# Attention as 64x64 quarter-array products of one head and two images (ViT tower, one core)

## What is computed

```python
B, N, D, H, DH = (64, 17, 256, 16, 64)       # images, tokens, width, heads, head width
q = (x @ Wq).reshape(b, n, H, DH)            # k, v alike
bias = slope[:, None, None] * (pos[:, None] - pos[None, :])
scores = jnp.einsum('bihd,bjhd->bhij', q, k) * scale + bias[None]
scores = jnp.where(causal[None, None], scores, jnp.float32(-1e+30))
attn = jax.nn.softmax(scores, axis=-1)
out = jnp.einsum('bhij,bjhd->bihd', attn, v).reshape(b, n, H * DH)
return out @ Wo + bo
```

## Time and profile before

| | before |
|---|---|
| median of 3 runs | 598.27 us (597.21 to 599.42) |
| profiled execution: time / span | 600.16 us / 598.4 us |
| mean granted TensorE clock | 0.918 |
| PE busy (MATMUL) / PE weight loads | 502.0 us (84%) / 405.5 us (68%) |
| DVE / ACT / GpSimd busy | 432.8 / 336.7 / 218.1 us |
| score products, L911: MATMUL records | 512, from 211.0 to 321.8 us |
| value products, L944: MATMUL records | 512, from 229.1 to 338.8 us |

### The profile page before, as it was taken

One profiled execution on the slowest core, in us unless ns is written; L12 is line 12 of the kernel. 1 busy time (PEld: TensorE's weight loads), 2 busy tenths in 40 slices (PEclk: granted clock), 3 DMA queues, 4 the chain that ended last, 5 costly groups with the idle time before them and its releaser, 6 DMA issues.

```text
span 598.4 us, 10880 instructions
## 1 busy us (share of the span) xinstructions
PE 502.0 (84%) x3750; PEld 405.5 (68%) x3754; DVE 432.8 (72%) x995; ACT 336.7 (56%) x798; POOL 218.1 (36%) x230
## 2 busy tenths in 40 slices
PE   3988953175654899999998998989999999999795
PEld 2756842033322789999998887867777777777584
DVE  4988998999999366666666323757686777766665
ACT  1588625245554867777775247336676767767500
POOL 2110001022222622222221522376777777777500
PEclk9996987577875899999999999999999999999969
DMA  8990000007400000000000010106777778887492
GB/s 266 380 359 0 1 0 0 0 2 250 115 2 1 1 27 29 28 29 28 27 2 3 1 53 23 29 13 191 225 219 217 219 229 237 232 240 213 133 398 80
DMA packets 43897, 67.36 MB, mean 113 GB/s; under 512 B 11022, under 2 KB 27015, under 8 KB 43716
## 3 DMA queue, kind: packets, MB, share of 16 engines
q1 hardware_dynamic: 36868, 64.62, 33.9%
q0 software_dynamic: 6976, 2.07, 1.8%
HBM read 66.81 MB, written 17.20 MB: 140 GB/s over the span
## 4 chain that ended last, share of the span: by engine, by line
PE 60%; DVE 24%; ACT 5%; issue 4%; DMA 3%; POOL 2%; SPq 0%; DVEq 0%; POOLq 0%; ACTq 0%
PE ps L1090 11%; PE ps L733 7%; PE ps L735 6%; PE ps L734 6%; PE ps L954 5%; PE ps L740 5%; PE ps L911 3%; PE ps L944 3%; PE ps L1080 3%; PE ps L926 2%; PE ps L1137 2%; PE ps L1098 2%; DVE region L1727 2%; DMA region<-x_rows,region 2%; DVE region L1738 2%
## 5 line engine op out<-in xcount | busy, mean ns | idle before, releaser
L1090 PE MATMUL ps<-region 128*128 128x352 f32 x256 | 86.4, 460 | 0.3 <-issue 0.3
L684 POOL DMA_INDIRECT region<-x_rows,region x64 | 67.9, 1061 | 20.2 <-issue 15.8
L733 PE MATMUL ps<-nTh,high 128*128 128x272 f32 (+2 forms) x248 | 73.7, 297 | 0.4 <-ACT region L1365 0.4
L734 PE MATMUL ps<-nTl,high 128*128 128x272 f32 (+2 forms) x248 | 71.1, 287 | 0.0
L693 POOL DMA_INDIRECT y_rows<-region x60 | 61.9, 1031 | 21.0 <-issue 14.4
L1783 DVE TENSOR_TENSOR region<-ps,region 32x136 f32<-32x136 f32 x128 | 38.1, 297 | 39.0 <-PE ps L911 37.5
L643 POOL COPY region<-region 32x544 f32<-32x544 f32 x32 | 26.1, 815 | 95.2 <-DVE region L1802 93.7
L1931 DVE SCALAR_TENSOR_TENSOR region<-region,ps 128x176 f32<-128x176 f32 x64 | 25.4, 397 | 44.7 <-ACT region L1442 42.9
L735 PE MATMUL ps<-nTh,pairs_low 128*128 128x272 f32 x192 | 55.0, 287 | 0.0
L1090 PEld LDWEIGHTS ps<-region 128*128 128x128 f32 x256 | 43.6, 190 | 14.1 <-issue 0.5
L1452 ACT ACTIVATE high<-region 88x512 fp32r<-88x512 f32 x64 | 40.4, 631 | 22.5 <-PE ps L735 21.5
(11 more groups left out here) (264 smaller groups left out, 1329.8 us busy)
## 6 DMA issues: line engine op xcount, KB each, us to landing
region<-moe_w SPq DMA_DIRECT2D x64, 352.0 KB, 3.9
region<-moe_w SPq DMA_DIRECT2D x64, 176.0 KB
y_rows<-zrow SPq DMA_DIRECT2D x1, 6528.0 KB, 25.5
region<-y_rows SPq DMA_DIRECT2D x8, 768.0 KB, 10.6
region<-wqkv SPq DMA_DIRECT2D x8, 384.0 KB, 3.0
region<-ffn_w SPq DMA_DIRECT2D x2, 1024.0 KB, 8.2
region<-patches SPq DMA_DIRECT2D x3, 384.0 KB, 8.3
region<-patches SPq DMA_DIRECT2D x1, 1152.0 KB, 10.7
```

What stands on the lines that cost most here:

```text
L684: nc.gpsimd.indirect_dma_start(out=xb[m8], out_offset=None, in_=x_rows, in_offset=bass.IndirectOffsetOnAxis(ap=sloti[:, at:at + 1], axis=0 ...
L733: nc.tensor.matmul(out, parts_a[0], parts_b[0], start=first, stop=False)
L734: nc.tensor.matmul(out, parts_a[0], parts_b[1], start=False, stop=False)
L1090: mm = nc.tensor.matmul(ps[:, 2 + m % 2, 0:2 * EI], xbT[m % 2][:, c, :], w13[m][:, c, :], start=(c == 0), stop=(c == DC - 1))
```

## The change

The score products become products of one head and two images: 64 partitions, 64 stationary and 34 moving columns. The keys are kept as they come out of the projection (`kT`), without zeros. Each half of the scores has its own two banks, one per head. The value products become products of one head and two images as well: 64 partitions (two images x 32 padded keys), 64 stationary and 34 moving columns, with `pbd` block-diagonal over two images; two banks are filled at a time, one per pair of images. There are twice as many products, each a quarter of the array. ACT's, DVE's and GpSimd's addresses follow. The `reg2.cut` lines without a name keep the places of the other buffers.

```diff
-        kbd = reg2.cut([P, GT, 2, GW])
+        kT = reg2.cut([P, N])
+        reg2.cut([P, 2 * GT * GW - N])
...
-        pbd = [reg2.cut([P, 2 * GT, GW]) for _ in range(2)]
+        pbd = [reg2.cut([P, 2 * GT, 2 * T]) for _ in range(2)]
+        reg2.cut([P, 2 * GT * GW])
...
-            nc.gpsimd.memset(kbd, 0.0).then_inc(s_zero, 1)
...
-            pool.wait_ge(s_zero, 6)
+            pool.wait_ge(s_zero, 5)
...
-                    nc.gpsimd.tensor_copy(pbd[j][r, :, q * T:(q + 1) * T], prT[r, :, 0:T]).then_inc(s_spread, 1)
+                    nc.gpsimd.tensor_copy(pbd[j][r, :, (q % 2) * T:(q % 2 + 1) * T], prT[r, :, 0:T]).then_inc(s_spread, 1)
...
                     def scores(half):
 
-                        need(pe, s_ext, 2 * n + half)
+                        need(pe, s_ext, 2 * n + half - 1)
                         for g in range(8):
                             t = 8 * half + g
-                            for u in range(2):
-                                mm = nc.tensor.matmul(ps[64 * u:64 * u + 64, 4 + g // 2, (g % 2) * GW:(g % 2 + 1) * GW].rearrange(
-                                                          "p (h w) -> p h w", h=2),
-                                                      qT[:, 4 * t + 2 * u:4 * t + 2 * u + 2, :].rearrange("p b t -> p (b t)"),
-                                                      kbd[:, t, :, 2 * u * T:2 * (u + 1) * T], start=True, stop=True)
+                            for hd in range(2):
+                                f = slice(DH * hd, DH * hd + DH)
+                                for u in range(2):
+                                    b = 4 * t + 2 * u
+                                    mm = nc.tensor.matmul(ps[64 * u:64 * u + 64, 4 + 2 * half + hd, 2 * g * T:2 * (g + 1) * T],
+                                                          qT[f, b:b + 2, :].rearrange("p b t -> p (b t)"),
+                                                          kT[f, b * T:(b + 2) * T], start=True, stop=True)
                         mm.then_inc(s_qk, 1)
...
-                    for g in range(4):
-                        if project and g == 2:
+                    for half in range(2):
+                        if project and half == 1:
                             scores(1)
-                        b = fill(g if not project else 16 + g)
-                        for k in range(4):
-                            for hd in range(2):
-                                f = slice(DH * hd, DH * hd + DH)
-                                mm = nc.tensor.matmul(ps[f, b, k * GW:(k + 1) * GW], vp[1 - j][:, 4 * g + k, f],
-                                                      pbd[1 - j][:, GT * hd + 4 * g + k, :], start=True, stop=True)
-                        mm.then_inc(s_fill, 1)
+                        at = 2 * half if not project else 16 + 2 * half
+                        banks = (fill(at), fill(at + 1))
+                        for k in range(8):
+                            for u in range(2):
+                                r = slice(64 * u, 64 * u + 64)
+                                for hd in range(2):
+                                    f = slice(DH * hd, DH * hd + DH)
+                                    mm = nc.tensor.matmul(ps[f, banks[u], 2 * k * T:2 * (k + 1) * T],
+                                                          vp[1 - j][r, 8 * half + k, f],
+                                                          pbd[1 - j][r, GT * hd + 8 * half + k, :], start=True, stop=True)
+                                if k == 7:
+                                    mm.then_inc(s_fill, 1)
...
-                            for hd in range(2):
-                                f = slice(DH * hd, DH * hd + DH)
-                                ins = nc.scalar.activation(kbd[f, 4 * q:4 * q + 4, hd, :],
-                                                           ps[f, q, 0:CW].rearrange("p (g w) -> p g w", w=GW), ACT.Copy)
-                            ins.then_inc(s_evac, 1)
+                            nc.scalar.activation(kT[:, q * CW:(q + 1) * CW], src, ACT.Copy).then_inc(s_evac, 1)
...
-                        nc.scalar.activation(attnT[:, n - 1, 4 * g * GW:4 * (g + 1) * GW], ps[:, g, 0:4 * GW],
-                                             ACT.Copy).then_inc(s_evac, 1)
+                        half, u = g // 2, g % 2
+                        nc.scalar.activation(
+                            attnT[:, n - 1, 8 * half * GW:8 * (half + 1) * GW].rearrange("p (k u w) -> p k u w", k=8, u=2)[:, :, u, :],
+                            ps[:, g, 0:16 * T].rearrange("p (k w) -> p k w", k=8), ACT.Copy).then_inc(s_evac, 1)
...
-                                sc[r, s0:s0 + 8, 0:T].rearrange("p (a b) t -> p a b t", a=4),
-                                ps[r, 4:8, 0:2 * GW].rearrange("p a (b h t) -> p a b h t", b=2, h=2)[
-                                    :, :, :, hd, (q % 2) * T:(q % 2 + 1) * T],
-                                bc(bc(bias[r, :], 1, 2), 1, 4), ALU.add)
+                                sc[r, s0:s0 + 8, 0:T],
+                                ps[r, 4 + 2 * half + hd, 0:16 * T].rearrange("p (g w) -> p g w", g=8)[
+                                    :, :, (q % 2) * T:(q % 2 + 1) * T],
+                                bc(bias[r, :], 1, 8), ALU.add)
```

More of the change, by code:

```diff
@@ L918, in attention @@
                     if n == 0:
-                        pe.wait_ge(s_zero, 6)
+                        pe.wait_ge(s_zero, 5)
                     scores(0)
@@ L1806, in _ @@
             low_parts(2, 0, len(groups))
-            dve.wait_ge(s_zero, 6)
+            dve.wait_ge(s_zero, 5)
             dve.wait_ge(s_wo1, 48)
```

## The result

The changed kernel takes 605.0 us (median of 6 runs, 603.07 to 607.65) where the kernel before takes 598.24 (6 runs, 596.79 to 599.42): ratio 1.0114, 95% interval 1.0096 to 1.0131. The forecast was 595.0 in a range of 591 to 623: the time is inside the range and on the other side of no change.

What follows compares the result with a forecast made beforehand. The attention loop was taken as bound by TensorE's own stream; -2.4 - 0.8 - 0.6 + 0.45 = -3.3 us on the profiled 600.16 gave 596.9, with the median 1.9 lower: 595.0 beside 598.27, range 591 to 623.

Steps and rivals of the forecast that it cites:

- R2: Score and value blocks: instruction feed gives 17 to 19 ns a pair, block 1.1 to 1.2 us, 602 to 605; chance 0.13.
- (a): Score and value blocks: 16 slots of 55 ns, 0.88 us instead of 0.94, with shorter block ends: -2.4 us together.
- R1: Score and value blocks: row halves take turns, 32 slots, 1.76 us a block, 623 us; chance 0.14.
- R2b: Score and value blocks: feed already at its limit, 29 ns a pair, 1.86 us a block, 626 us; chance 0.06.
- R4: Score and value blocks: load quicker in a quarter tile, down to 30 ns a slot, 583 us; chance 0.05.
- R3: Score and value blocks: tiles overlap but the slot stays near 59 ns, nothing measurable, 597 us; chance 0.12.
- (b): Scores half 1 of n=0: a bank pair per half removes the wait for DVE's read of half 0: -0.8 us.
- (c): Keys leave PSUM in four copies instead of eight, shortening PE's waits for ACT at n=1: -0.6 us.
- (d): Drain pass: value blocks free two banks at their end, so PE waits for two copies instead of one: +0.45 us.
- (e): POOL's clearing before attention is about 3.8 us shorter, its copies and DVE's reads move as much as before: nothing.

Runs made afterwards that it cites:

- one-image run: The changed kernel with 17 moving columns a product instead of 34, the odd image of each pair not computed: 609.98 us, one execution, beside before's 597.93.
- shifted kernel: The changed kernel with 64 transposes of a bf16 identity (128 instructions) added where TensorE waits for DVE, long before attention: 605.48 us, ratio 1.011.
- two joined versions: Kernel before with two banks per scores half, both halves behind the twelfth projection group: 0.9978; the same with quarter scores and keys without zeros: 0.9941.
- values alone: Kernel before with the changed kernel's quarter value products, probabilities and attnT copies, scores and keys as before: 603.18 us, ratio 1.0081.
- scores alone: Kernel before with the changed kernel's quarter scores, keys and DVE reads, value products as before: 598.66 us, ratio 0.9998.

## Why the prediction was wrong, step by step

**The step that failed is the feed of instructions.** The sum puts it at nothing; it stands beside the sum as R2. The prediction saw that the change needs a pair per 14 ns, and asked of the trace only how fast TensorE takes the pairs of one block; it gave this 0.13, as an even slowing to 17 to 19 ns a pair. The runs showed in its place two rates: within a piece of instructions the feed keeps up with 14.5 ns a pair (128 pairs in 1.85 us), and pieces of 256 instructions cannot follow each other faster than some 3.5 us. So nothing is slower in most blocks, and 0.5 to 2.2 us is lost at once in others. That R2's 602 to 605 holds the measured 605.0 is luck: the mechanism is another. A row that could have raised the question was on the page of before and wasn't read, the instruction queue. It shows how many pieces come, not how fast they could; the same stretch, 240 to 256 us, in before and then in after:
```profile
q8 instruction: 1, 0.02, 0.5%
```
```profile
q8 instruction: 3, 0.05, 1.3%
```
Before needs 436 instructions an iteration of 15.1 us, after 693 (both counted in the traces). On average 693 would still arrive in 9.5 us; it is the run of 384 within 2.8 us that outruns them. What makes the next piece start is open: in the changed kernel's attention it mostly starts 0.6 to 1.6 us after TensorE enters a new piece, but sometimes before that, and once 3.1 us after. That one belongs to the longest stop, 2.23 us at 261.55: the last piece had been entered at 257.9, and the next packet started only at 261.0. So I can't say ahead which iteration stops.

**(a), the blocks, -2.4 forecast, none measured.** The mechanism was right: four quarter tiles overlap, 16 slots a block. The size was off: 58 ns a slot, not 55, so 0.93 us a block, where the forecast had 0.88 and the kernel before 0.94 to 0.95. The two block ends of an iteration gave some 20 to 30 ns each, as forecast: score block to transposes is 1.07 instead of 1.10 us, the last value block to the projections 1.07 instead of some 1.11. So the four blocks of an iteration took 0.09 us less, not 0.30. And the rest took it back: an undisturbed iteration is 15.12 to 15.19 us against 15.12; the projections with their neighbours took 9.20 us (232.21 to 241.41) instead of 9.13, which no run explains. The one-image run shows that the forecast's reason, streaming sets 59 and the load 55, was half wrong: with 17 columns the slot is 58 too, so the stream does not set it, and whatever does costs 58 and not 55. The load itself is as forecast, a median of 135 ns with 64 rows, 136 with 128. By the Trainium skill ("TensorE: Matmul & The Clock Gate", LDWEIGHTS (loading the stationary operand)) it goes with columns only; the trace agrees.

R1 (turns, 1.76 us a block) and R2b (1.86) fall to the same 0.93, R4 too. The floor of about 25 ns between MATMUL starts that the Trainium skill gives ("TensorE: Matmul & The Clock Gate", "Wait — 56ns, not 53.3ns?") does not hold for four tiles: 64 starts in 0.93 us are 14.5 ns apart. R3's place, a slot near 59, is what the array part did.

**(b), n = 0, -0.8 forecast.** Transposes to scores half 1 is 1.90 us (212.23 to 214.13) instead of 2.74: -0.84. Right.

**(c), the keys, -0.6 forecast.** The rest of the first iteration's -1.49, -0.65; the stop of 0.67 us before L733 at n = 1 is gone. The two joined versions differ by it again, 13.90 and 13.23. L1371's 32 copies take 397 ns each. The size is right, the reading under it was not: "1.0, 2" in the earlier trace rows is not two places but one, where a load waited 0.60 us and its product 0.38 of the same time. 0.67 us from record to record, of which 0.13 is the product's own, was all there was at this place.

**(d), +0.45 forecast.** The last block to L962 in the drain pass: 0.99 us (348.67 to 349.66) instead of 0.72, +0.27. Right in kind. What was missed is n = 7: the wait there went from DVE to ACT's L1384, since the stop of 1.68 us had given DVE its time; last value record to L962 took 1.07 us instead of 1.90, so the stop cost only part of its length: the stretch was +0.82, and +0.21 in the shifted kernel, which has no stop there.

**(e), nothing.** POOL and DVE were never late. Right.

Right terms alone, -0.84 - 0.65 + 0.27 = -1.2, would have been no measurable change. The six stops, 9.0 us less what their products take anyway, and two stretches at the lower clock, 3.3, made it slower. How much of the clock's part belongs to the supply is argued, not shown: the clock fell behind a stop of 2.23 us and behind two of 1.68 and 1.07 close together, it fell behind n = 7's wait of 1.78 with values alone, but not behind before's 1.90 or the shifted kernel's 2.14 at the same place.

## What to carry to other kernels

Before cutting products into smaller tiles, count instructions as well as columns: here TensorE got 256 per 3.5 us at best, and runs of 256 to 384 instructions, used at 256 in 1.9 us, stopped in the middle of a block in some iterations, with "issue" as the only name for it and the instruction queue's packets as the witness. Halving what a product streams gained nothing, neither from 68 to 34 columns nor from 34 to 17: the slot stayed at 58 to 59 ns. What did pay was the half of the change with the shorter runs: a bank set for each half and both score halves in front of the transposes (0.2% with before's products), and with them quarter scores on keys without zeros (0.6% in all), the values left as they were. That version has one run of 256 instructions an iteration and did not stop in its eight iterations; scores alone in before's order, with a run of 256 too, stopped once.

## What the runs showed of the hardware that was not expected

- The supply: 16 KB a packet, 3.5 to 3.75 us from one to the next when TensorE is waiting, and 1.2 to 1.6 us from a packet's landing to the end of the stop, in all 26 stops. Each stop ends at an instruction whose number in the stream leaves the same remainder when divided by 256.
- Four fp32 quarter tiles take a pair of load and MATMUL per 14.5 ns, whether 34 or 17 columns are streamed.
- Two blocks of unlike tile shape back to back lose 0.13 to 0.16 us at the seam (1.06 and 1.10 against 0.93 and 0.94 us a block), 0.24 us an iteration with two seams more.
- Nine satisfied waits (four instructions) behind each product of TensorE: a product every 0.44 us instead of every 0.059.
